# Filling TensorE's array in the convolution, loading the down weights ahead, and reordering the attention loop of a three-part block

## The reference

```python
xs = gelu(x @ W1.T + b1)                       # 192 -> 48 channels
xs = abs(ifft2(mask * fft2(xs)))               # fixed low-pass over the 16 x 16 positions
x = x + xs @ W2.T + b2                         # 48 -> 192 channels

n = layernorm(t)                               # attention: scores stand between the
q, k, v = n @ Wq + bq, n @ Wk + bk, n @ Wv + bv  # 12 heads of one token, k and v have one head
q, k = rope(q), rope(k)
attn = softmax(einsum('bsid,bsjd->bsij', q, k) / 4)
t = t + einsum('bsij,bsjd->bsid', attn, v)

n = layernorm(t)                               # mixture of 8 experts, top 2
p = softmax(n @ gate_w.T); choose 2, renormalise
y_e = (silu(n @ gate_bank[e]) * (n @ up_bank[e])) @ down_bank[e]
t = t + sum over the chosen e of p_e * y_e
```

## Time and profile before

| | |
|---|---|
| runs | 475.07, 470.65, 477.8 us; median 475.07 |
| profiled execution | 475.46 us, span 473.7 us, mean granted clock 0.88 |
| busy in the span | PE 394.8 us (83%), PEld 373.5, DVE 276.5, POOL 280.7, ACT 222.0 |
| DMA | 41.27 MB, mean 87 GB/s |
| costliest lines | L1078 POOL x72, 114.6 us busy; L1070 POOL x72, 70.5 us busy |

### The profile page before, as it was taken

One profiled execution on the slowest core, in us unless ns is written; L12 is line 12 of the kernel. 1 busy time (PEld: TensorE's weight loads), 2 busy tenths in 40 slices (PEclk: granted clock), 3 DMA queues, 4 the chain that ended last, 5 costly groups with the idle time before them and its releaser, 6 DMA issues.

```text
span 473.7 us, 9033 instructions
## 1 busy us (share of the span) xinstructions
PE 394.8 (83%) x2236; PEld 373.5 (79%) x2237; DVE 276.5 (58%) x718; ACT 222.0 (47%) x513; POOL 280.7 (59%) x302
## 2 busy tenths in 40 slices
PE   5799954779888585176789999999999999999990
PEld 5799943668777474065689999999999999999990
DVE  1265683387667622997156666666666666666650
ACT  3434420434555441085245555555565556555550
POOL 0256561277777642001637877887878788787753
PEclk9999999976888555555689999999999999999996
DMA  7998532003333534200314444444445444444442
GB/s 213 245 230 227 145 68 63 25 1 103 104 102 116 148 99 137 24 0 12 104 21 68 75 78 68 72 79 72 72 73 79 68 72 77 70 73 74 59 44 25
DMA packets 46087, 41.27 MB, mean 87 GB/s; under 512 B 14153, under 2 KB 40108, under 8 KB 46060
## 3 DMA queue, kind: packets, MB, share of 16 engines
q0 software_dynamic: 14016, 17.21, 22.8%
q1 hardware_dynamic: 32044, 23.75, 18.9%
HBM read 25.87 MB, written 15.08 MB: 86 GB/s over the span
## 4 chain that ended last, share of the span: by engine, by line
PE 48%; DMA 2%; issue 1%; another core or an unknown queue 1%; ACT 0%; POOLq 0%; DVE 0%; SPq 0%; ACTq 0%; DVEq 0%
PE moe_ps_y L1137 8%; PE moe_ps_h L1123 5%; PE moe_ps_gt L1112 3%; PE moe_ps_gt L1116 3%; PE moe_ps_gt L1113 3%; PE moe_ps_gt L1115 3%; PE moe_ps_gt L1114 3%; PE moe_ps_u L1112 3%; PE moe_ps_y L1139 3%; PE moe_ps_u L1113 3%; PE moe_ps_u L1114 3%; PE moe_ps_u L1115 3%; PE moe_ps_u L1116 3%; PE moe_ps_x L1104 2%; PE moe_ps_x L1103 2%; PE moe_ps_y L1136 2%
## 5 line engine op out<-in xcount | busy, mean ns | idle before, releaser
L1078 POOL DMA_INDIRECT out<-moe_y,idx_map x72 | 114.6, 1592 | 39.8 <-issue 20.2
L1070 POOL DMA_INDIRECT moe_xt<-rows,idx_map x72 | 70.5, 979 | 55.7 <-POOLq L865 34.0
L1213 ACT ACTIVATE moe_yy<-moe_ps_y,moe_xt 128x384 f32<-128x384 f32 x72 | 41.9, 583 | 71.9 <-PE moe_ps_y L1137 58.0
L1137 PE MATMUL moe_ps_y<-wd,moe_h_hi 128*128 x216 | 71.6, 356 | 0.7 <-DVE moe_h_lo L1275 0.5
L1283 DVE TENSOR_TENSOR moe_y<-moe_yy 128x192 f32<-128x192 f32 x72 | 25.8, 359 | 57.1 <-ACT moe_yy L1213 47.7
L1193 ACT ACTIVATE moe_x_hi<-moe_ps_x 128x256 fp32r<-128x256 f32 x72 | 27.7, 385 | 38.2 <-PE moe_ps_x L1104 32.1
L1275 DVE TENSOR_TENSOR moe_h_lo<-moe_ps_h,moe_h_hi 128x384 fp32r<-128x384 f32 x72 | 40.2, 559 | 5.7 <-ACT moe_h_hi L1205 3.6
L1137 PEld LDWEIGHTS moe_ps_y<-wd,moe_h_hi 128*128 128x128 f32 x216 | 41.3, 191 | 1.3 <-issue 1.3
L1269 DVE TENSOR_TENSOR moe_hid<-moe_ps_u,moe_sg 128x384 f32<-128x384 f32 x72 | 39.4, 548 | 1.2 <-issue 1.2
L1259 DVE TENSOR_TENSOR moe_x_lo<-moe_ps_x,moe_x_hi 128x128 fp32r<-128x128 f32 x72 | 21.0, 292 | 31.8 <-ACT moe_x_hi L1193 25.3
L1205 ACT ACTIVATE moe_h_hi<-moe_ps_h 128x384 fp32r<-128x384 f32 x72 | 35.5, 493 | 4.0 <-remote 2.4
(11 more groups left out here) (188 smaller groups left out, 1124.2 us busy)
## 6 DMA issues: line engine op xcount, KB each, us to landing
xs<-in_x SPq DMA_DIRECT2D x8, 384.0 KB, 5.1
conv_stage<-in_wgu SPq DMA_DIRECT2D x8, 384.0 KB, 3.8
conv_stage<-in_wgu SPq DMA_DIRECT2D x16, 192.0 KB, 4.6
rows<-attn_xr SPq DMA_DIRECT2D x8, 384.0 KB, 2.7
out<-xs SPq DMA_DIRECT2D x8, 384.0 KB, 3.4
attn_stage<-in_down SPq DMA_DIRECT2D x8, 288.0 KB, 3.4
conv_xta<-in_xT SPq DMA_DIRECT2D x8, 256.0 KB, 4.3
moe_xt<-rows,idx_map POOLq DMA_INDIRECT x72
```

The costliest lines, as they stand in the source:

```text
L1070: nc.gpsimd.indirect_dma_start(xt[:, slot, :], None, rows.ap(), bass.IndirectOffsetOnAxis(ap=idx_map[:, j, 0:1], axis=0)).then_inc(gathere ...
L1078: nc.gpsimd.indirect_dma_start(out, bass.IndirectOffsetOnAxis(ap=idx_map[:, j, 1:2], axis=0), y[:, j % YR, :], None, compute_op=ALU.add).t ...
L1137: ins = nc.tensor.matmul(both, hi, halves, start=(k == 0), stop=(k == 2))
L1213: nc.scalar.activation(yy[:, s].rearrange("p h c -> p (h c)"), ps_y[:, s, 0:2 * C], ACT.Copy, scale=xt[:, slot, bass.ds(GC + e, 1)]).then_ ...
```

## The change

In the convolution the two halves of W1 lie in tiles of 128 columns with zeros beyond the 48, and `in_product` moves all 128; the two parts of the magnitude of one image lie under one another in one tile `yt_hl` (high part in the 64 rows of the image, low part in the other 64), the rows of W2 are in the tile twice with zeros between, and `out_product` is 8 matmuls of 128 rows. For that DVE clears the tiles first and SP's first transfers wait for it. ACT writes the magnitude once in full and once per half, DVE subtracts per half. The down weights of all 8 experts are loaded at the end of the convolution straight to where their low part will be; ACT makes all 8 high parts after the first transposes' copy, POOL 5 low parts ahead of the first rotation and one in each of the first three quads. ACT's exponential stands ahead of `norm_route`, POOL's `weigh_value` ahead of the deviation. The expert phase has 71 tiles.

```diff
-TILES_MAX = -(-(2 * TOKENS // P + EXPERTS - 1) // XR) * XR
+TILES_USED = 2 * TOKENS // P + EXPERTS - 1
+TILES_MAX = -(-TILES_USED // XR) * XR
 GC = C + CB
...
         yt = a.sb("yt", [P, RING, SEQ])
-        yt_hi, yt_lo = a.sb("yt_hi", [P, RING, SEQ], F32R), a.sb("yt_lo", [P, RING, SEQ], F32R)
+        yt_hl = a.sb("yt_hl", [P, RING, 2, SEQ], F32R)
...
         g_lo_done, yt_lo_done = a.sem("g_lo_done"), a.sem("yt_lo_done")
-        g_made = a.sem("g_made")
+        g_made, w2_filled, wide = a.sem("g_made"), a.sem("w2_filled"), a.sem("wide")
         pool_turn, dve_turn = a.sem("pool_turn"), a.sem("dve_turn")
         with nc.Block() as block:
             @block.sync
             def _(sp):
-                sp.dma_start(w1a[:], w1[0:P, :]).then_inc(w1_in, 16)
-                sp.dma_start(w1b[:], w1[P:C + 1, :]).then_inc(w1_in, 16)
+                sp.wait_ge(wide, 2)
+                sp.dma_start(w1a[:, 0:DH], w1[0:P, :]).then_inc(w1_in, 16)
+                sp.dma_start(w1b[:, 0:DH], w1[P:C + 1, :]).then_inc(w1_in, 16)
...
                 sp.dma_start(lp[:], lowpass.rearrange("(h p) s -> p h s", p=P)).then_inc(consts_in, 16)
+                sp.wait_ge(w2_filled, 1)
                 sp.dma_start(w2s[0:DH + 1, :], w2).then_inc(consts_in, 16)
...
                     sp.dma_start(dst, src).then_inc(later_in, 16)
+                for e in range(EXPERTS):
+                    sp.dma_start(wd[:, e, :, 1, :].bitcast(F32),
+                                 down[e].rearrange("(k p) c -> p k c", p=P)).then_inc(down_in, 16)
                 sp.wait_ge(later_in, 16 * len(later))
...
                     for t in range(QT):
-                        at = ps_w1[:, s, t * DH:(t + 1) * DH]
+                        at = ps_w1[:, s, t * P:(t + 1) * P]
                         nc.tensor.matmul(at, xta[:, s, bass.ts(t, P)], w1a[:], start=True, stop=False)
...
                     for m in range(2):
-                        k = slice(DP * m, DP * m + DH + 1)
                         for h in range(2):
                             at = ps_c[:, s, m, h * C:(h + 1) * C]
-                            hi, lo = yt_hi[k, s, bass.ts(h, P)], yt_lo[k, s, bass.ts(h, P)]
-                            nc.tensor.matmul(at, hi, w2_hi[k, :], start=True, stop=False)
-                            nc.tensor.matmul(at, hi, w2_lo[k, :], start=False, stop=False)
-                            last = nc.tensor.matmul(at, lo, w2_hi[k, :], start=False, stop=True)
+                            both = yt_hl[:, s, m, bass.ts(h, P)]
+                            nc.tensor.matmul(at, both, w2_hi[:], start=True, stop=False)
+                            last = nc.tensor.matmul(at, both, w2_lo[:], start=False, stop=True)
                     last.then_inc(w2_done, 1)
...
                     nc.scalar.activation(g[:, s].rearrange("p h m d -> p m h d")[:, :, :, 0:DH],
-                                         ps_w1[:, s, 0:QT * DH].rearrange("p (m h d) -> p m h d", m=2, h=2),
+                                         ps_w1[:, s].rearrange("p (m h d) -> p m h d", m=2, h=2)[:, :, :, 0:DH],
                                          ACT.Gelu).then_inc(g_made, 1)
...
                     act.wait_ge(yt_lo_done, freed(q))
-                    for dst in (yt, yt_hi):
-                        ins = nc.scalar.activation(dst[:, s, :], ps_f[:, s, 0:SEQ], ACT.Abs, bias=y_bias[:, 0:1])
+                    nc.scalar.activation(yt[:, s, :], ps_f[:, s, 0:SEQ], ACT.Abs, bias=y_bias[:, 0:1])
+                    for m in range(2):
+                        b = slice(DP * m, DP * (m + 1))
+                        ins = nc.scalar.activation(yt_hl[b, s, m, :], ps_f[b, s, 0:SEQ], ACT.Abs, bias=y_bias[b, 0:1])
                     ins.then_inc(abs_done, 1)
...
             def _(dve):
+                nc.vector.memset(w1a[:], 0.0).then_inc(wide, 1)
+                nc.vector.memset(w1b[:], 0.0).then_inc(wide, 1)
                 nc.vector.memset(xtb[CB:CB + 1, :, :], 1.0).then_inc(bias_row, 1)
+                nc.vector.memset(w2s[:], 0.0).then_inc(w2_filled, 1)
                 dve.sem_inc(added, RING)
...
                 nc.vector.tensor_tensor(lp_lo[:], lp[:], lp_hi[:].bitcast(F32), ALU.subtract)
-                for k in (0, DP):
-                    b = slice(k, k + DH + 1)
-                    ins = nc.vector.tensor_tensor(w2_lo[b, :], w2s[b, :], w2_hi[b, :].bitcast(F32), ALU.subtract)
-                ins.then_inc(const_lo_done, 1)
+                nc.vector.tensor_tensor(w2_lo[:], w2s[:], w2_hi[:].bitcast(F32),
+                                        ALU.subtract).then_inc(const_lo_done, 1)
...
                     dve.wait_ge(w2_done, freed(q))
-                    nc.vector.tensor_tensor(yt_lo[:, s], yt[:, s], yt_hi[:, s].bitcast(F32),
-                                            ALU.subtract).then_inc(yt_lo_done, 1)
+                    for m in range(2):
+                        b, o = slice(DP * m, DP * (m + 1)), slice(DP * (1 - m), DP * (2 - m))
+                        ins = nc.vector.tensor_tensor(yt_hl[o, s, m, :], yt[b, s], yt_hl[b, s, m, :].bitcast(F32),
+                                                      ALU.subtract)
+                    ins.then_inc(yt_lo_done, 1)
...
-                def load_weights(i, s):
-                    q = quad(i, s)
-                    sp.wait_ge(lo_done, freed(q))
-                    sp.dma_start(stage[:, s].rearrange("p (k c) -> p k c", k=3),
-                                 down[q].rearrange("(k p) c -> p k c", p=P)).then_inc(stage_in[s], 16)
-
                 def store(i, s):
...
-                load_weights(0, 0)
-                load_weights(0, 1)
-                with sp.Fori(1, QUADS // RING) as i:
+                with sp.Fori(0, QUADS // RING) as i:
                     for s in range(RING):
-                        load_weights(i, s)
-                        store(i - 1, s)
-                for s in range(RING):
-                    store(last, s)
+                        store(i, s)
                 sp.wait_ge(stored, 16)
...
-                def split(i, s):
-                    act.wait_ge(stage_in[s], 16 * i + 16)
-                    nc.scalar.activation(wd[:, quad(i, s), :, 0, :], stage[:, s].rearrange("p (k c) -> p k c", k=3),
-                                         ACT.Copy).then_inc(hi_done, 1)
+                def split(e):
+                    nc.scalar.activation(wd[:, e, :, 0, :], wd[:, e, :, 1, :].bitcast(F32), ACT.Copy).then_inc(hi_done, 1)
...
                 out_of_psum(0, 0)
+                act.wait_ge(down_in, 16 * EXPERTS)
+                for e in range(EXPERTS):
+                    split(e)
                 for n in range(QUADS + LAG_OUT):
...
                     if n < QUADS:
-                        split(*turned(0, n))
+                        exponential(*turned(0, n))
                     if 0 <= n - RING < QUADS:
                         norm_route(*turned(0, n - RING))
-                    if n < QUADS:
-                        exponential(*turned(0, n))
             @block.gpsimd
             def _(pool):
-                for c in (lo_done, pow_done, eps_done, mean_done, dev_done, kk_done, pv_done):
+                for c in (pow_done, eps_done, mean_done, dev_done, kk_done, pv_done):
                     pool.sem_inc(c, RING)
...
-                def split(i, s):
-                    q = quad(i, s)
-                    pool.wait_ge(hi_done, made(q))
+                def split(e):
+                    pool.wait_ge(hi_done, e + 1)
                     pool.sem_inc(pool_turn, 1)
-                    nc.gpsimd.tensor_tensor(wd[:, q, :, 1, :], stage[:, s].rearrange("p (k c) -> p k c", k=3),
-                                            wd[:, q, :, 0, :].bitcast(F32), ALU.subtract).then_inc(lo_done, 1)
+                    low = wd[:, e, :, 1, :]
+                    nc.gpsimd.tensor_tensor(low, low.bitcast(F32), wd[:, e, :, 0, :].bitcast(F32), ALU.subtract)
...
+                for e in range(EXPERTS - 3):
+                    split(e)
                 rotate_key(0, 0)
-                split(0, 0)
                 for n in range(QUADS):
                     if n + 1 < QUADS:
                         rotate_key(*turned(0, n + 1))
+                    weigh_value(*turned(0, n))
                     if n:
                         deviation(*turned(0, n - 1))
-                    weigh_value(*turned(0, n))
-                    if n + 1 < QUADS:
-                        split(*turned(0, n + 1))
+                    if n < 3:
+                        split(EXPERTS - 3 + n)
                 deviation(last, 1)
...
         N = TILES_MAX
+        REST = TILES_USED - (N - XR)
...
                     gather(j)
-                for j in range(N):
+                for j in range(TILES_USED):
                     scatter(j)
-                    if j + AHEAD < N:
+                    if j + AHEAD < TILES_USED:
                         gather(j + AHEAD)
...
                 sp.wait_ge(meet_done, 1)
```

(4 more changed lines are left out.)

51 lines of the change are left out of this document (23 added, 28 removed).

## The result

Twenty runs of each kernel: 467.86 us median (464.65 to 470.47) against 475.67 (470.65 to 479.81). The ratio is 0.985, with a 95% interval of 0.982 to 0.988, so the change saves 7.2 us (5.8 to 8.5); forecast were 10.7. (The medians are of all runs; the ratio leaves out those more than 1.5% above the fastest of the same kernel, which is why it gives a little less than the 7.8 us between them.) The time lies in the range. The direction is the one forecast, though 7.2 us is under the 2% that were called faster. Inside that sum one step was wrong in sign, as the experiments show.

What follows compares the result with a forecast made beforehand. Bounds: loads, then PE at 1.2 GHz in the convolution; POOL's order in the attention; PE in the expert phase. Convolution -4.5, attention -3.2, tile -3.0 from 475.46 give 464.8, on the median 464.6; range 457 to 472 us.

Steps and rivals of the forecast that it cites:

- The convolution, -4.5: Convolution: clock rises for a good part, loads then bind, half of 9.1 us standing DMA won; -4.5 us (-7 to -1).
- The rule cited from the Trainium skill: Convolution clock: steady matmul activity alone releases full clock, so widening changes nothing in it; sum 3.3 us higher.
- Down weights at no cost: Down weights: loads land before ACT asks, splits fit in idle time of ACT and POOL; cost nothing.
- The attention loop, period 9.65, -4.2: Attention loop: weigh_value ahead of the deviation on POOL shortens the period from 10.5 to 9.65; five periods, -4.2 us.
- The 0.6 ahead of the loop: Ahead of the attention loop: ACT's split no longer stands before an exponential; -0.6 us.
- rival D: Attention loop: PE loses full clock, 13.6 us copy to copy in place of 10.5, five quads +15.5; 487 us, chance 0.06.
- Rival C: Attention loop gives nothing back: deviation's slow instruction stays at 2.07 us beside DVE's residual; 468.3 us, chance 0.17.
- The tail, +1.6: Behind the attention loop: quad 5's deviation is later by weigh_value, and the router's last transposes follow; +1.6 us.
- The tile, -3.0: End of the expert phase: without the last scatter the kernel ends on the one ahead; -3.0 us (-3.2 to -2.5).
- rival B: Convolution stays at 1.2 GHz, since PE fully busy did not raise the clock; 467.9 us, chance 0.22.
- 9.4 and no return: Attention's lower bound: loop period 9.4 us and no +1.6 given back behind the loop; -6.5 us.
- 10.5 and the return: Attention's upper bound: loop period stays 10.5 us and the tail gives back +1.6; stated as +1.6 us.

Runs made afterwards that it cites:

- the kernel with 48 columns: Convolution's part alone on the kernel before, but its first product moves 48 columns again, stacked operands kept; ratio to before 0.997 (0.993 to 1.001).
- the one with 128 columns: The kernel before with the convolution's part of the change alone; ratio to before 0.988 (0.983 to 0.994).
- the old order with the added matmul: Changed kernel with deviation ahead of weigh_value, full-operand tail, and one unread 240-column matmul ahead of each quad's projections; ratio to before 0.969 (0.964 to 0.973).

## Why the prediction came out as it did

- **The convolution, -4.5**: right. 5.5 measured alone (2.7 to 8.3), 3.8 at the start of the attention. The widened product cost nothing at 1.2 GHz, as said: its pairs of instructions start 0.43 us apart with 128 columns as with 48. The clock rose in about half of the distances, and PE then waited for its loads, as forecast. What the step did not have is that the matmuls behind such a wait are at 1.2 GHz again (49.91 above). The rule cited from the Trainium skill ("TensorE: Matmul & The Clock Gate", Part 1, "What's actually happening") would have left the clock as it was. The traces disagree with it once more: from 40 to 60 us the kernel with 48 columns is busy 19.99 of 20 us at a granted clock of 0.52, the one with 128 columns 13.02 of 20 at 0.90.
- **Down weights at no cost**: right; ACT's and POOL's splits lie in the waits named. What was not costed is the good side of it: the split left POOL's loop, and DVE's residual fell from 2.0 to 0.96 us. That is what makes 8.9 us a quad possible.
- **The attention loop, period 9.65, -4.2**: wrong. The chain was named correctly (rotation, `weigh_value`, deviation, `norm_route`, copy) and measured at 9.93: the forecast gave `weigh_value` its old 1.63 us, though in its new place it meets DVE's scores and takes 1.95. That is 0.3 a quad. The larger error is what it was compared with. The 10.5 of the one trace isn't the old order's length: in the three other traces with it most quads take 9.9 to 10.1 and one or two take 10.6 to 10.9, so its loop (first to eighth copy) is 66.5 us in the mean of four. The new order has 68.4 in the mean of three, since each has one quad of 12.8 or 12.9 with projections and logits at 1.2 GHz. The 0.6 ahead of the loop did come: from the first copy to the second it is 6.42 us against 7.12.
- **The rivals of this step.** The slow quad is rival D, priced at 13.6 a quad and given 0.06 for five quads; it comes in one. Why it comes stays open. In the new order PE's transposes for the router wait for the later `norm_route`, but that this pause is the cause was not tried by itself, and the old order with the added matmul had such a quad too (12.73 us). Rival C is nearest in its number for the attention, but its cause did not occur: the deviation's slow instruction takes 1.04 us in its new place (115.51 above), not 2.07.
- **The tail, +1.6**: right, 1.55: 32.85 and 32.86 us in the two traces with this order and the old tail, against 31.3 in four before.
- **The tile, -3.0**: right, 3.5 (1.7 to 5.3).
- **Sum**: -10.7 forecast, -7.2 measured. With the attention at +2.6 in place of -3.2 the forecast's own terms would have given -4.9; the convolution gave 1 more and the tile 0.5. That the number came this near is in part luck, since these two made up for part of the attention's error; without them the time would be 470.2, near the upper end of the range. The median of 467.86 is also the number of rival B (467.9) and close to C's (468.3), and neither is what happened. The chance of 0.17 for an attention that gives nothing was too low, and the right comparison, the changed kernel with the old order, wasn't among the cases.
- **Two bounds do not follow from their periods.** With 9.4 and no return the attention's term is 5 x 1.1 + 0.6 = 6.1, not 6.5; with 10.5 and the return it is -0.6 + 1.6 = +1.0, not +1.6. The measured +2.6 lies beyond either.

## What to carry to other kernels

When several edits meet in one loop, cost each against the loop that the others leave behind: removing the split had already freed 1.1 us a quad, and the reordering written for the loop with the split spent them. Before moving an instruction on one engine, look at what the other engine does at its new place, and at which engine's chain then holds all steps in a row. A stretch in which TensorE is never idle can still run at 1.2 GHz (busy 20.00 of 20 us before, 0.21 us from one 256-column matmul to the next); the distance between two starts of equal matmuls shows it, and operands padded with zeros to the full array can be the cheaper ones.

## What the runs showed that I had not expected

The recorded clock of the kernel before says 1.00 in the convolution while its matmuls run at 1.2 GHz; in the changed one it is 0.80 from 40 to 60 us and agrees with the distances. Identical code in the expert phase took 240.1 to 245.6 us in ten executions, and the loop of the attention took 65.7 to 67.7 us with the same code in four, so a single pair of traces settles nothing under 5 us here. And in the tail 128 moved columns are cheaper than 8 even at 1.2 GHz: the instruction pairs start 0.43 us apart (164.01 to 164.44 above) where those of 8 columns start 0.52 apart (166.48, 167.01, 167.53 in the changed kernel). Every second pair also fills 128 rows in place of 64; the 0.43 and the 0.52 are the same for both kinds.
